# Block one-hots compared from broadcast rows, gates scaled by ScalarE, and the gate layers moved one turn back

## The reference

```python
gate = jax.nn.silu(edge_attr @ F1W + F1b) @ F2W + F2b
...
cw = jnp.where(distances < CUT, 0.5 * (jnp.cos(jnp.pi * distances / CUT) + 1.0), 0.0)
...
msg = gate * h[dst] * (cw * mj)[:, None]
agg = jax.ops.segment_sum(msg, src, num_segments=N)
```

## Time and profile before

| | us |
|---|---|
| runs, median (lowest to highest of 3) | 14316.78 (14309.37 to 14319.74) |
| the profiled execution, its own time | 14305.02 |
| its span | 14303.3 |
| ranking loop, first to last L1143 | 402.8 to 2779.6 |
| PE, DVE, ACT, POOL busy over the span | 81%, 85%, 57%, 51% |

### The profile page before, as it was taken

The page is one execution under the profiler, slowest core; times in us unless marked ns, Lnnn a source line. Parts: engine busy times, 40 slices in busy tenths (PEclk is TensorE's granted clock), DMA queues, the critical chain, the costliest instruction groups (busy, mean ns, idle before and its releaser), DMA issues.

```text
span 14303.3 us, 630454 instructions
## 1 busy us (share of the span) xinstructions
PE 11578.7 (81%) x196113; PEld 9877.2 (69%) x196113; DVE 12194.2 (85%) x29979; ACT 8167.6 (57%) x26006; POOL 7231.4 (51%) x9217
## 2 busy tenths in 40 slices
PE   2899999986765888988987988988997767686566
PEld 2666666775665877777776877777776666576556
DVE  5788888767898899988998899988998889699997
ACT  0344444345676688867886788867885302067630
POOL 0566666634453654535553655545552355565436
PEclk9999999999855955576555955586555678685586
DMA  9322222464797877757774877757775976589957
GB/s 381 99 60 60 60 60 60 52 101 156 273 286 210 308 189 190 190 186 248 190 190 124 311 189 190 187 208 231 193 193 174 304 204 218 146 293 282 248 190 204
DMA packets 3472139, 2731.34 MB, mean 191 GB/s; under 512 B 2332483, under 2 KB 3076116, under 8 KB 3471750
## 3 DMA queue, kind: packets, MB, share of 16 engines
q1 hardware_dynamic: 2746678, 1045.93, 29.0%
q0 software_dynamic: 236192, 860.68, 20.7%
q10 hardware_dynamic: 489008, 821.78, 15.4%
HBM read 1616.59 MB, written 1110.81 MB: 191 GB/s over the span
## 4 chain that ended last, share of the span: by engine, by line
PE 26%; DVE 25%; DMA 14%; issue 14%; ACT 10%; DVEq 5%; SPq 4%; ACTq 1%; POOL 1%; POOLq 0%
DMA chunk_layer_rows<-arena 7%; DVE arena L1886 6%; PE ps L1160 5%; PE ps L1151 5%; ACT arena L1021 4%; DVE arena L1813 3%; DMA arena<-edge_hot_b 3%; PE ps L1307 3%; PE ps L1342 2%; DVEq L109 2%; PE ps L1274 2%; PE ps L1143 2%; ACT arena L847 2%; PE ps L1180 2%; DVE arena L1791 2%
## 5 line engine op out<-in xcount | busy, mean ns | idle before, releaser
L1307 PE MATMUL ps<-arena 128*128 128x49 bf16 x56160 | 2596.5, 213 | 879.7 <-DVE arena L1829 421.0
L1307 PEld LDWEIGHTS ps<-arena 128*128 128x128 fp8e4 x56160 | 2336.1, 115 | 1193.8 <-issue 1182.8
L1274 PE MATMUL ps<-block_tables,arena 128*128 128x98 bf16 (+2 forms) x56160 | 2449.2, 201 | 603.0 <-DVE arena L1799 305.9
L1274 PEld LDWEIGHTS ps<-block_tables,arena 128*128 128x128 bf16 (+1 forms) x56160 | 2220.6, 99 | 831.9 <-issue 394.6
L743 POOL COPY block_tables<-arena 128x294 bf16 (+2 forms) x2340 | 1445.1, 618 | 2211.1 <-PE ps L1274 1293.2
L957 ACT ACTIVATE arena<-ps 128x392 f32<-128x392 f32 (+1 forms) x3900 | 1711.5, 480 | 1053.1 <-PE ps L1274 640.7
L705 POOL DMA_INDIRECT edge_records<-arena x1563 | 1558.9, 997 | 1227.3 <-DVE arena L1585 834.5
L727 POOL DMA_INDIRECT arena<-chunk_layer_rows,map_a x1040 | 1043.2, 1003 | 2018.8 <-ACT arena L1021 1929.7
L1021 ACT ACTIVATE arena<-arena,small 128x49 f32<-128x49 f32 x8320 | 1996.8, 323 | 102.1 <-ACT small L1013 0.7
L1799 DVE TENSOR_SCALAR arena<-arena,iota_row 128x1024 bf16<-128x1024 uint8 x2080 | 1567.4, 754 | 113.7 <-PE ps L1274 60.7
L1886 DVE CUSTOM_DVE_ANT_0 arena<-ps,arena 128x1024 bf16<-128x1024 f32 x1040 | 1273.4, 1224 | 321.4 <-PE ps L1342 211.0
(11 more groups left out here) (323 smaller groups left out, 20530.3 us busy)
## 6 DMA issues: line engine op xcount, KB each, us to landing
chunk_layer_rows<-arena ACTq DMA_DIRECT2D x1040, 392.0 KB, 3.3
arena<-node_hot_a SPq DMA_DIRECT2D x1820, 128.0 KB
arena<-edge_hot_a SPq DMA_DIRECT2D x1560, 128.0 KB
chunk_gated<-arena ACTq DMA_DIRECT2D x520, 324.0 KB, 2.7
arena<-edge_records SPq DMA_DIRECT2D x1040, 160.0 KB
chunk_rows<-arena ACTq DMA_DIRECT2D x780, 196.0 KB, 2.0
arena<-edge_records SPq DMA_DIRECT2D x520, 196.0 KB
arena<-edge_hot_b SPq DMA_DIRECT2D x780, 128.0 KB
```

What stands on the lines that cost most here:

```text
L1274: last = pe.matmul(psv[:, 2 * r + j // tpb, (j % tpb) * w:(j % tpb + 1) * w], hot[:, s, j * P:(j + 1) * P], bt4[:, s, i, 0:w], start=i == ...
L1307: last = pe.matmul(to[s % 2], he4j[:, s % 4, j, :], low_part(i, s, j), start=j == 0 and i == 0, stop=j == C8 - 1 and i == 2)
```

## The change

- The transposed one-hots are no longer made on PE. Ahead of the loop, after the first counting step, PE transposes the block numbers of all edges (26 transposes), ACT copies them to SBUF in the middle of its filler stores, and SP stores them as rows in DRAM (four DMAs). In the loop SP's new step `load_blocks` broadcasts the 512 block numbers of the group over 49 partitions, once for sources and once for destinations; DVE's new step `turned` compares them with the partition's own block number. PE's `turn` and ACT's `turned` are gone.
- `gates` moves from DVE (two operations) to ACT (eight copies with a scale, one for each gate and column).
- The lags: PE's `mlp_1` from 1 to 2, `mlp_2` from 2 to 3; ACT's `mlp2` from 1 to 2, `fill` from 0 to 2, `gates` at 3.
- `update` waits for the one-hots itself; the staged semaphores count four DMAs a group instead of two.

```diff
--- before.py
+++ after.py
@@ -45,6 +45,7 @@
 CC = 16
 NCC = -(-NQ * CQ // (2 * CC)) * 2
 ET = NCC * CC
+NBC = -(-NQ * CQ // P)
 RW = 139
 C_KS, C_G1, C_CUT, C_G2 = 40, 42, 90, 91
 G1_0, G2_0 = 42, 90
@@ -157,6 +158,7 @@
         row_a = dram("key_rows_a", [NT, P], U8)
         row_b = dram("key_rows_b", [NT, P], U8)
         hot_na = dram("node_hot_a", [NS * P, BT], U8)
+        blk_row = [dram(n, [NQ * CQ, P], BF16) for n in ("source_blocks", "destination_blocks")]
         hot_ea = dram("edge_hot_a", [NS * P, BT], U8)
         hot_eb = dram("edge_hot_b", [NS * P, BT], U8)
         kdc = dram("dst_keys_a", [P * (NS + 1), C8])
@@ -291,12 +294,14 @@
         nul = prep(ROWG + C8)
         io_st = prep(NS)
         sels = prep(3 * NS)
+        sdb = prep(4 * CQ * P // 2, BF16)
         astr = prep(2 * NS)
         ddt = prep(2 * NS)
         aend = prep(P)
         aidx = prep(NS)
         valid = prep(NS)
         pieces = arena[:, src_at:src_at + 2 * KPIECE * P]
+        blk_rows = arena[:, src_at:src_at + 2 * NBC * P // 2].bitcast(BF16).rearrange("p (k t c) -> p k t c", k=2, c=P)
         wm_t, wub, wmu = (prep(L * H) for _ in range(3))
         ioi = prep(1024, I32)
         sel_f = prep(2 * 1024)
@@ -554,6 +560,11 @@
             sp.wait_ge(cleared, 8)
             sp.dma_start(xs3[:, 0:NB - 1, :], a["x"][0:(NB - 1) * P, :].rearrange("(b p) c -> p b c", p=P)).then_inc(nodes_loaded, 16)
             sp.dma_start(xs3[0:LAST, NB - 1, :], a["x"][(NB - 1) * P:N, :]).then_inc(nodes_loaded, 16)
+            last_c = (NBC - 1) * P
+            for k in range(2):
+                sp.wait_ge(blk_evac, 2 * k + 2)
+                sp.dma_start(blk_row[k][0:last_c, :].rearrange("(t i) c -> i t c", i=P), blk_rows[:, k, 0:NBC - 1, :]).then_inc(blk_stored, 16)
+                sp.dma_start(blk_row[k][last_c:NQ * CQ, :], blk_rows[0:NQ * CQ - last_c, k, NBC - 1, :]).then_inc(blk_stored, 16)
             for c in range(NS // 20):
                 sp.dma_start(rec_flat[c * 20:c * 20 + 10].rearrange("s p c -> p s c"),
                              pad.unsqueeze(1).to_broadcast([P, 10, C8 * RW])).then_inc(pads_stored, 16)
@@ -561,6 +572,14 @@
             sp.dma_start(ww[H:W96, :], wmu[0:H, :]).then_inc(wmu_done, 16)
 
             stg4 = stg.rearrange("p (u j c) -> p u j c", u=U, c=RW)
+
+            sdb4 = sdb.rearrange("p (u c) -> p u c", u=4)
+
+            def load_blocks(k, s):
+                if not (isinstance(k, int) and k < 4):
+                    hold(sp, "sp", (q["te"], k - 3))
+                for i, row in enumerate(blk_row):
+                    sp.dma_start(sdb4[i * NB:(i + 1) * NB, s, :], row.rearrange("(k t) c -> k (t c)", t=CQ)[bass.ds(k, 1), :].squeeze(0).partition_broadcast(NB)).then_inc(ea_staged[s], 16)
 
             def load_ea(k, s):
                 hold(sp, "sp", (q["filled"], 3 * k - 9), (q["eat"], k - 3))
@@ -569,7 +588,8 @@
                     sp.dma_start(ea_p4[rows, s, 0:w, 0, :],
                                  edges_of.rearrange("(p t) c -> p t c", t=n)[:, bass.ds(k * CQ, w), :]).then_inc(ea_staged[s], 16)
 
-            walk(nc, sp, NQ, [(0, load_ea)])
+            sp.wait_ge(blk_stored, 64)
+            walk(nc, sp, NQ, [(0, load_blocks), (0, load_ea)])
 
             for s in range(U):
                 sp.wait_ge(scattered[s], all_scattered(s))
@@ -807,6 +827,15 @@
         def _(act):
             act.wait_ge(cleared, 1)
             for c in range(NS // 20):
+                if c == 4:
+                    for k in range(2):
+                        for i in range(2):
+                            act.wait_ge(blk_turned, 2 * k + i + 1)
+                            n = (8, NBC - 1 - 8)[i]
+                            got = act.activation(blk_rows[:, k, 8 * i:8 * i + n, :], psb[:, 4 + 2 * k + i, 0:n * P].rearrange("p (t c) -> p t c", c=P), ACT.Copy)
+                        w = NQ * CQ - (NBC - 1) * P
+                        got.then_inc(blk_evac, 1)
+                        act.activation(blk_rows[0:w, k, NBC - 1, :], psb[0:w, 5 + 2 * k, (NBC - 9) * P:(NBC - 8) * P], ACT.Copy).then_inc(blk_evac, 1)
                 act.dma_start(rec_flat[c * 20 + 10:c * 20 + 20].rearrange("s p c -> p s c"),
                               pad.unsqueeze(1).to_broadcast([P, 10, C8 * RW])).then_inc(pads_stored, 16)
             act.wait_ge(angle_ready, 1)
@@ -816,17 +845,9 @@
             act.activation(wmu[0:H, :], psv[0:H, 6, 0:L * H], ACT.Copy).then_inc(wmu_done, 1)
 
             stg4 = stg.rearrange("p (u j c) -> p u j c", u=U, c=RW)
-            sdt2 = sdt.rearrange("p (u c) -> p u c", u=2)
             eat2 = eat.rearrange("p (u t c) -> p u t c", u=2, c=P)
             hid2 = hid.rearrange("p (u c) -> p u c", u=2)
             ksd3 = ksd.rearrange("p (t c) -> p t c", c=2)
-
-            def turned(k, s):
-                r = s % 2
-                act.wait_ge(q["t"], k + 1)
-                wait(act, q["look"], k - 1)
-                hot = psb[:, 0, r * 512:(r + 1) * 512].rearrange("p (t c) -> p t c", c=P)[:, :, 0:P]
-                act.activation(sdt2[0:2 * NB, r, :].rearrange("p (t c) -> p t c", c=P)[:, :, 0:P], hot[0:2 * NB], ACT.Copy).then_inc(q["te"], 1)
 
             def counts(k, s):
                 r = s % 2
@@ -835,7 +856,7 @@
                 act.activation(mp[0:NB, r, 0, :], psv[0:NB, 3, 0:CQ * NB], ACT.Copy).then_inc(q["mcp"], 1)
 
             def fill(k, s):
-                hold(act, "act", (scattered[s], (k - s) * (16 * CQ // U)), (ea_staged[s], (k - s) * (32 // U) + 32))
+                hold(act, "act", (scattered[s], (k - s) * (16 * CQ // U)), (ea_staged[s], (k - s) * (64 // U) + 64))
                 act.activation(stg4[0:P, s, :, 0:R], ea_p4[0:P, s, :, 0, :], ACT.Copy, scale=0.1).then_inc(q["filled"], 1)
                 act.activation(stg4[0:P, s, :, C_KS:C_KS + 2], ksd3[0:P, bass.ds(k * CQ, CQ), :], ACT.Copy).then_inc(q["filled"], 1)
                 act.activation(stg4[0:P, s, :, C_CUT], w_e[0:P, bass.ds(k * CQ, CQ)], ACT.Copy).then_inc(q["filled"], 1)
@@ -852,10 +873,19 @@
                 wait(act, q["g"], k - 1)
                 act.activation(hid2[0:W96, r, :], psv[0:W96, 5, 0:CQ * P], ACT.Silu, bias=fb1[:, 0:1]).then_inc(q["act"], 1)
 
+            def gates(k, s):
+                r = s % 2
+                hold(act, "act", (q["g"], k + 1))
+                for at_, of in ((C_G1, 0), (C_G2, H)):
+                    for j in range(CQ):
+                        last = act.activation(stg4[0:P, s, j, at_:at_ + H], psv[0:P, 6 + r, j * W96 + of:j * W96 + of + H], ACT.Copy,
+                                              scale=w_e[0:P, bass.ds(k * CQ + j, 1)])
+                    last.then_inc(q["kept"], 1)
+
             act.wait_ge(params_loaded, PARAMS * 16)
             act.wait_ge(cut_ready, 1)
             act.wait_ge(off["base"], 1)
-            walk(nc, act, NQ, [(1, counts), (1, mlp2), (0, fill), (0, turned), (0, mlp1)])
+            walk(nc, act, NQ, [(1, counts), (2, mlp2), (2, fill), (3, gates), (0, mlp1)])
 
             keys3 = ksd_l.rearrange("p (s j c) -> p s j c", j=C8, c=2)
             for s in range(U):
@@ -1076,6 +1106,13 @@
             pe.wait_ge(off_v["begins"], 1)
             pe.matmul(psv[0:NB, 3, 0:CQ * NB], ident[0:NB, 0:NB], m0[0:NB, :], start=True, stop=False, skip_group_check=True)
             count(0, 0)
+            kkh = kk.bitcast(BF16).rearrange("p (t k h) -> p t k h", k=2, h=2)
+            for k in range(2):
+                for c in range(NBC):
+                    w = min(P, NQ * CQ - c * P)
+                    last = pe.transpose(psb[0:w, 4 + 2 * k + c // 8, (c % 8) * P:(c % 8 + 1) * P], kkh[:, c * P:c * P + w, k, 1], identb[:, :])
+                    if c in (7, NBC - 1):
+                        last.then_inc(blk_turned, 1)
             count(1, 1)
             with pe.Fori(1, NCC // 2) as i:
                 for u in range(2):
@@ -1093,6 +1130,7 @@
             pe.matmul(psv[0:NB, 3, 0:CQ * NB], ident[0:NB, 0:NB], m0[0:NB, 0:CQ * NB], start=True, stop=False,
                       skip_group_check=True).then_inc(off["base"], 1)
             pe.wait_ge(params_loaded, PARAMS * 16)
+            pe.wait_ge(blk_evac, 4)
             for l in range(L):
                 last = pe.matmul(psv[0:H, 6, l * H:(l + 1) * H], wm_t[0:H, l * H:(l + 1) * H], wub[0:H, l * H:(l + 1) * H],
                                  start=True, stop=True)
@@ -1101,14 +1139,6 @@
             sdt2 = sdt.rearrange("p (u t c) -> p u t c", u=2, c=P)
             eat2 = eat.rearrange("p (u t c) -> p u t c", u=2, c=P)
             hid2 = hid.rearrange("p (u t c) -> p u t c", u=2, c=P)
-
-            def turn(k, s):
-                r = s % 2
-                pe.wait_ge(q["sd"], k + 1)
-                wait(pe, q["te"], k)
-                for t in range(CQ):
-                    last = pe.transpose(psb[0:2 * NB, 0, r * 512 + t * P:r * 512 + t * P + P], sd4v[0:P, s, t, :], identb[:, :])
-                last.then_inc(q["t"], 1)
 
             def row(k, s):
```

(32 more changed lines are left out.)

## The result

The changed kernel takes 14099.3 us (median of 4 runs, 14074.54 to 14105.93) beside 14313.1 us for the kernel before (4 runs, 14292.33 to 14319.74): ratio 0.985, 95% interval 0.9833 to 0.9867. The forecast was 14088. The medians lie 214 us apart and the two profiled executions 230 (14074.5 for the kernel after), where the sum gave 229. That holds for the chip of this comparison. On two others the changed kernel is the slower one, at 1.0198 (1.0181 to 1.0215) and 1.0189 (1.0172 to 1.0206) of the kernel before; the last group of experiments is about that.

What follows compares the result with a forecast made beforehand. PE was taken to bound the ranking loop: 390 turns shortened from 6.094 to 5.48 us save 239 us, less 10 is 229, giving 14076 from the profiled 14305.0 and 14088 us as median. The range was 14020 to 14230.

Steps and rivals of the forecast that it cites:

- the sum: Ranking loop's turn falls from 6.094 to 5.48 us; 390 turns save 239 us, less 10 is 229.
- PE, the main term: Ranking loop: without the transposes and the wait for ACT, PE needs 5.45 us a turn, between 5.39 and 5.65.
- The two halves: Ranking loop on PE: removing the transposes saves 0.43 us; longer lags remove the wait for ACT's 0.61 us copy.
- No wait gained: Ranking loop on PE: upper bound of 5.65 us a turn, 6.08 less 0.43, if only the transposes' time goes.
- DVE: Ranking loop: without gates 4.93 us a turn, plus 0.49 for the compare, 5.42; from 5.22 to 5.62.
- The near tie: Ranking loop: DVE's 5.42 us lies just under PE's 5.45, so 0.03 us a turn was added.
- ACT: Ranking loop: its work rises from 2.51 to 3.83 us a turn, at most 4.5, with 0.6 us of slack.
- Rival 3: Ranking loop: slow gates on ACT make PE wait again; 14150 to 14327 us, middle 14210, chance 0.08.
- POOL: Ranking loop: four scatters take 5.2 us a turn, below 5.45; cover shrinks from 0.9 to 0.25 us.
- Loads, prologue, drain: Loop loads need 4.3 of about 10.6 us, hidden; work ahead of the loop costs 5 us, the extra turn 5.
- Rivals 1 and 2: Ranking loop: DVE's compare and POOL's scatters block each other; 14197 us, chance 0.17, or at worst 14444 us, chance 0.05.
- Rival 4: Ranking loop: TensorE runs at 2.4 instead of 1.2 GHz; 13980 to 14066 us, middle 14025, chance 0.08.

Runs made afterwards that it cites:

- the last group of experiments: Kernels before and after rerun unchanged, and two variants, on chips with stalls; the changed kernel took 15609.9 and 15592.9 us, 1.0198 and 1.0189 of the kernel before.
- rows_only: Changed kernel with the old lags and gates back on DVE, leaving only the broadcast rows and compare; 15454.9 us, 1.0154 of the kernel before.
- lags_only: Kernel before with only the gate layers' lags lengthened, transposes on PE and gates on DVE kept; 15441.3 us, 1.015 of the kernel before.
- old_lags: Changed kernel with the old lags put back, broadcast rows and gates on ACT kept; 15109.8 us in one run.
- two_products_b: Changed kernel with the third, smallest matmul product of mlp_1 left out; 15534.8 us, 1.0153 of the kernel before on that chip.
- tt_compare_b: Changed kernel with turned comparing two full tiles instead of a tile against a per-partition scalar; 15402.2 us, 1.0059 of the kernel before on that chip.

## Why the prediction was right, and where it wasn't

*PE, the main term.* The mechanism came as described: PE alone sets the turn. 5.45 was taken, 5.48 in the sum, 5.51 came. Timeline of PE of the kernel after, last matmul of `look` and the next `mlp_1`:

```profile
1510.24 0.23 PE L1159 MATMUL ps<-arena 49*128 49x49 bf16 x1
1510.40 0.66 PE L1181 MATMUL ps<-arena,f_parts 120*96 120x512 bf16 x1
```

The hand-over is 0.16 us where 0.06 + 0.06 was given, and the rest of this turn is 5.55 - 0.16 = 5.39 where 5.33 was taken (5.76 - 0.43); three turns of four are 0.05 shorter than this one. The 0.03 added for DVE covered half of the miss, for another reason.

*The two halves.* "No wait gained" was put at 5.65, and the parts were added as if neither needed the other. The quick turns bear this out: 5.63 in `rows_only` without `turn`, and 0.15 for the distances in `lags_only`. What the prediction didn't say is that the gates on ACT need the distances; with the old ones they take the ring back to 5.94 (`old_lags`).

*DVE.* 5.42 was too much. `turned` took 0.340 us, 0.26 from its start to the next one's, not 0.49; the nearest rows had other sizes. DVE waited for PE for (118.5 + 12.3)/374 = 0.35 us a turn, so it needs at most 5.16, and the ring in `two_products_b` gives 5.07. The near tie didn't exist. With the gates still on it DVE needs 5.27, so their move to ACT was not what kept DVE out of the way. The Trainium skill (VectorE: DVE Perf Modes, "What auto-detection actually checks") has `turned` at four elements a cycle, and a compare of two tiles at two. The trace agrees in the direction: 0.340 us against 0.414 for the same size in `tt_compare_b`, about half of the 0.13 us that was estimated from the page's clock.

*ACT.* Gates: 611.1/2985 = 0.205 us each of busy time (0.24 taken), and ACT waits for PE in every turn, 352.5 us before L881 in this stretch, 0.94 a turn. Rival 3 has no piece in the chain.

*POOL.* 5.2 was taken and its lengthening left out: 5.43 with issue. By this sum, not by a run, most of any further gain on PE's side would have been lost to POOL. The 0.5 us of idle before a turn's first scatter isn't there.

*Loads, prologue, drain.* No DMA piece stands in the chain of the loop. The prologue cost 5.1 us (5 taken), and the first work behind the loop comes 217 us sooner: 227, less 5.1 and about 4.6 for the drain (5 taken). The other 13 us up to 230 come after that, in code that both kernels share, and no term had them. So that 230 meets 229 is luck: the loop and its ends gave 12 us less than the sum, and the code behind them 13 more than nothing.

*Rivals 1 and 2.* A scatter and a DVE operation do get in each other's way, but the one that waits is POOL's: `turned` has no spread (0.340 us mean, nearly all within 0.335 to 0.348), while scatters that run into `ea_parts` behind `turned` grow to 1.42. POOL had room for that. The Trainium skill (SBUF — State Buffer, "Who interferes with whom") has the descriptor side starving behind such a compare. The trace agrees in which side waits, 0.97 against 1.42 us, but not in the trigger: the compare alone, 0.971, does nothing, and the scatters that wait end with L1587, a subtraction of two SBUF tiles.

*Rival 4.* Four 128-column matmuls (L1148) still take 0.43 us, 1.2 columns a ns: TensorE stayed at 1.2 GHz, as in the earlier trace rows. Half as many transposes brought no higher clock. The 1.00 that the table prints for the loop has no record behind it: the first clock record of this profile is at 3210.9 us, and at 3502.8 in that of before.

*What no step had.* That the sign could depend on the chip (or on what changed with the chips). Of the three chips on which both kernels ran side by side, the changed one is faster on one.

## What to carry to other kernels

A change made of three edits needs a run for each, and the length of each ring in it, before one of them is called necessary. Here the shorter PE work and the longer distances nearly add (0.45 and 0.15, and 0.58 together), and the third edit, the gates on ACT, makes the distances necessary without being needed itself, as far as these lengths tell: with it and the old distances most of the gain is gone (5.94), and DVE had room for the gates (5.27 of 5.51).

A quick turn between stalls is no rate of the kernel, but its chain of waits gives the length of the ring that it closes, and an engine that catches up without waiting shows its own need. Both are worth having where the total is spoiled.

A ring with every engine near its bound has little slack for an update that comes late, and in this case the lateness differed from chip to chip; measure such a change on more than one, and on the first again, before believing a gain of 1.5%. And when a total meets its forecast, add up the measured terms too: here two misses of 12 and 13 us cancelled.
